# Second layer as sixteen lagged rounds, with sums of probabilities on TensorE and their reciprocal on VectorE

## The chip, the cores and the metric

One core of a Trainium2 chip. The metric is the time of one execution of the whole program on the device, in microseconds (us); lower is better. Three runs of the kernel before took 2073.58, 2075.54 and 2075.81 us (median 2075.54).

## The reference

Three things are computed one after the other on x of 8 batches x 256 x 512, in float32: a first cross-attention layer with its own network; a second layer (the one that changes), which is a self-attention block and then a cross-attention block over `ctx_2048`; and a network. The second layer's attention, cut to what matters:

```python
def attention(q, k, v, mask):
    scores = einsum('bhqd,bhkd->bhqk', q, k) / sqrt(32)      # 16 heads of 32
    scores = scores * mask - 10000.0 * (1.0 - mask)
    probs = softmax(scores, axis=-1)
    return einsum('bhqk,bhkd->bhqd', probs, v)

h = layernorm(x) @ w_qkv            # 512 x 1536, self-attention, mask shared by the batches
x1 = x + attention(q, k, v, m_self) @ w_ao + b_ao
q = layernorm(x1) @ w_q; k, v = split(ctx @ w_kv)             # cross-attention, a mask per batch
x2 = x1 + attention(q, k, v, m_cross[b]) @ w_co + b_co
```

256 tokens per batch, so each (batch, block, head) has a 256 x 256 matrix of probabilities.

## The kernel before

The program builds three parts in turn: `first_layer` (tiles named a_), `attention_layer` (b_) and `network_layer` (c_). A block of instructions per engine is written out by hand, with semaphores between them; each engine works its own queue strictly in order. Only `attention_layer` is changed.

**Units.** A unit is four heads by 128 queries: 8 units for a batch in one block, 128 in all. A unit goes through: `scores` (TensorE, L1281, four matmuls of 96 stacked rows: q and k are split into a high and a low float32r part, written to DRAM by `put` and read back stacked by `stack`), `soften` (VectorE: L1499 times the mask out of PSUM, L1503 adds and takes the row maximum), `exponentials` (ScalarE, L1393, whose accumulator also gives the row's sum `esum`), `turn_probs` (TensorE, L1293, eight transposes), `keep` (ScalarE, L1405, copies them out of PSUM), `weigh` (TensorE, L1307, values times probabilities in four column strips of the array; then L1312 spreads the reciprocals of the sums over 128 x 128 by a matmul with the identity), `invert` (VectorE, L1511, reciprocal of 4 sums) and `divide` (VectorE, L1521 copies the spread reciprocals out, L1523 multiplies).

**Order.** A loop body stands for one batch, with sixteen positions p. At each position every engine does one step of three or four different units (scores of unit p+2, transposes of p, `weigh` of p-1) and one item of `FILL`: a bank's worth of projections, layer-norm transposes or output projection for another batch. The self units of batch i+1 and i+2 alternate with the cross units of batch i: a body holds 8 of either kind. Projections are plain float32: `project` (L1219, eight matmuls of 256 columns a bank) and `by_token` (L1227, four of 512 columns a bank). A float32 matmul stands in the records as two instructions, so the counts of rows on such lines are twice those of the code; a float32r one is one instruction.

**Buffers.** Four PSUM banks in turn for transposes, weighed values and fills, and four banks for the scores of two units (`score[:, u % 2]`). A bank is claimed anew when the reader of its use four places before is done (`claim`).

**The network after it** (c_) already works with float32r parts: each product of a high and low part is three matmuls (L1745 with 256 columns, L1759 with 512), the first times the low, the low times the first, and the two high ones.

Rows name an instruction by its line, its engine, what it writes `<-` what it reads, and partitions x elements.

Of the kernel before, what the change touches and what calls it, by code (L numbers as in the profile page):

```python
# [12 lines left out]
P = 128  # L13
BANK = 512
# [843 lines left out]
def attention_layer(nc, sems, hid, enc_in, masks, ident_in, W, mid_out, scratch):  # L858

    B, S, D = hid.shape
# [5 lines left out]
    HUGE = 3.0e38  # L868

# [8 lines left out]
    FIRST, LAST = -3, B  # L878
    POSITIONS = range(2 * NU)
# [6 lines left out]
    def there(b):  # L886
        return not isinstance(b, int) or 0 <= b < B

    def unit_at(i, p):

        if p < 0:
            return CROSS, i - 1, p + NU
        if p < NU:
            return SELF, i + 1, p
        if p < 2 * NU:
            return CROSS, i, p - NU
        return SELF, i + 2, p - 2 * NU

    def phase_before(a, b):
        if a == CROSS:  # L900
            return (CROSS, b - 1) if isinstance(b, int) and b == B - 1 else (SELF, b + 1)
        if isinstance(b, int) and b < 2:
            return (SELF, 0) if b == 1 else None
        return CROSS, b - 2

    def two_before(a, b, u):
        if u >= 2:
            return a, b, u - 2
        phase = phase_before(a, b)
        return phase and (*phase, u + NU - 2)  # L910

    def earlier(uses, at, step, i):

        while True:
            at -= step
            if at < 0:
                at, i = at + len(uses), i - 1
                if isinstance(i, int) and i < FIRST:
                    return None
            use, shift = uses[at]  # L920
            if use and there(i + shift):
                return use, i + shift

    with ExitStack() as ctx:
# [3 lines left out]
        def sig(name, per, unit=1):  # L928
            return Signal(sems, nc, "b_" + name, per, unit)

        wqkv = sb("wqkv", [P, KT, 3 * D])
        wkv = sb("wkv", [P, KT, 2 * D])
        wq2 = sb("wq2", [P, KT, D])
        wout = [sb(f"wout{a}", [P, KT, D]) for a in range(2)]
# [5 lines left out]
        bqs = sb("bqs", [P, 2, KT])  # L940
# [3 lines left out]
        mask = [sb(f"mask{a}", [P, TT, S]) for a in range(2)]  # L944
        minus = [sb(f"minus{a}", [P, TT, S]) for a in range(2)]
        xt = sb("xt", [P, TT, D])
        xb = sb("xb", [P, TT, D])
        x1 = sb("x1", [P, TT, D])
        x1b = sb("x1b", [P, TT, D])
        xn = sb("xn", [P, TT, D])  # L950
        enc = sb("enc", [P, TT, D])
        lnT = [sb(f"lnT{a}", [P, KT, S]) for a in range(2)]
        encT = sb("encT", [P, KT, S])
        stats = sb("stats", [P, 2, TT, 6])
        mv = sb("mv", [P, 2, TT, 2])
        vare = sb("vare", [P, 2, TT])
        rstd = sb("rstd", [P, 2, TT])
        full = [sb(f"full{s}", [P, KT, S]) for s in range(2)]
        parts = sb("parts", [P, 2, KT, S], F32R)
        qst = sb("qst", [ROWS, 2, HH, S], F32R)  # L960
        kst = sb("kst", [ROWS, 2, HH, S], F32R)
        val = [sb(f"val{a}", [P, TT, D]) for a in range(2)]
# [3 lines left out]
        esum = sb("esum", [P, NU, G])  # L966
        inverse = sb("inverse", [P, NU, G])
        spread = sb("spread", [P, 2, P])
        pt = sb("pt", [P, 2, TT, G * P])
        cxT = [sb(f"cxT{a}", [P, KT, S]) for a in range(2)]  # L970

        consts_in = sig("consts_in", 1, 16)
        qk_in = sig("qk_in", 1, 16)
        v_in = sig("v_in", 1, 16)
        mask0_in = sig("mask0_in", 1, 16)
        late_in = sig("late_in", 1, 16)
        x_in = sig("x_in", 1, 16)
        enc_load = sig("enc_load", 1, 16)
        mask_in = sig("mask_in", 1, 16)
        set_up = sig("set_up", 1)  # L980
        x_biased = [sig(f"x_biased{a}", 1) for a in range(2)]
        var_done = [sig(f"var_done{a}", 1) for a in range(2)]
        rstd_done = [sig(f"rstd_done{a}", 1) for a in range(2)]
        xn_done = [sig(f"xn_done{a}", 1) for a in range(2)]
        turn_filled = [sig(f"turn_filled{a}", 2) for a in range(2)]
        ln_done = [sig(f"ln_done{a}", KT) for a in range(2)]
        enc_filled = sig("enc_filled", 2)
        enc_done = sig("enc_done", 2)
        qk_filled = [sig(f"qk_filled{a}", 4) for a in range(2)]
        v_filled = [sig(f"v_filled{a}", TT) for a in range(2)]  # L990
        q_full = [sig(f"q_full{a}", KT) for a in range(2)]
        k_full = [sig(f"k_full{a}", KT) for a in range(2)]
        v_done = [sig(f"v_done{a}", TT) for a in range(2)]
        q_parts = [sig(f"q_parts{a}", 1) for a in range(2)]
        k_parts = [sig(f"k_parts{a}", 1) for a in range(2)]
        qk_out = [[sig(f"qk_out{a}{h}", 4, 16) for h in range(2)] for a in range(2)]
        stacked = [[sig(f"stacked{a}{h}", 2 * len(Q_PARTS), 16) for h in range(2)] for a in range(2)]
        score_filled = [sig(f"score_filled{a}", NU) for a in range(2)]
        masked = [sig(f"masked{a}", NU) for a in range(2)]
        max_done = [sig(f"max_done{a}", NU) for a in range(2)]  # L1000
        exp_done = [sig(f"exp_done{a}", NU) for a in range(2)]
        pt_filled = [sig(f"pt_filled{a}", NU * TT) for a in range(2)]
        pt_done = [sig(f"pt_done{a}", NU * TT) for a in range(2)]
        pv_done = [sig(f"pv_done{a}", NU) for a in range(2)]
        inverse_done = [sig(f"inverse_done{a}", NU) for a in range(2)]
        cx_done = [sig(f"cx_done{a}", NU) for a in range(2)]
        cxT_done = [sig(f"cxT_done{a}", KT) for a in range(2)]
        o_filled = [sig(f"o_filled{a}", TT) for a in range(2)]
        x_done = [sig(f"x_done{a}", TT) for a in range(2)]
# [4 lines left out]
            0: [(("turn", 0, u), 2) for u in range(2)],  # L1014
            1: [(("q", 0, 0), 2)],
            2: [(("o", 1, t_), -1) for t_ in range(TT)],
            3: [(("q", 0, 1), 2)],
            4: [(("k", 0, 0), 2)],
            5: [(("k", 0, 1), 2)],
            6: [(("v", 1, 0), 0)],  # L1020
            7: [(("v", 1, 1), 0)],
            8: [(("enc", u), 1) for u in range(2)],
            9: [(("k", 1, 0), 1)],
            10: [(("o", 0, t_), 1) for t_ in range(TT)],
            11: [(("k", 1, 1), 1)],
            12: [(("v", 0, 0), 2)],
            13: [(("turn", 1, u), 1) for u in range(2)] + [(("v", 0, 1), 2)],
            14: [(("q", 1, 0), 1)],
            15: [(("q", 1, 1), 1)],
        }  # L1030
        BANKS = 4
        uses = []
        for p in POSITIONS:
            a, shift, u = unit_at(0, p)
            uses += [(("pt", a, u, k), shift) for k in range(TT)]
            a, shift, u = unit_at(0, p - 1)
            uses += [(("w", a, u), shift)]
            uses += FILL[p]
        uses += [(None, 0)] * (-len(uses) % BANKS)
        place = {use: n for n, (use, _) in enumerate(uses) if use}  # L1040
        read = {("enc", u): (enc_done, u + 1) for u in range(2)}
        for a in range(2):
            read |= {("turn", a, u): (ln_done[a], 2 * u + 2) for u in range(2)}
            read |= {("q", a, u): (q_full[a], 2 * u + 2) for u in range(2)}
            read |= {("k", a, u): (k_full[a], 2 * u + 2) for u in range(2)}
            read |= {("v", a, t_): (v_done[a], t_ + 1) for t_ in range(TT)}
            read |= {("pt", a, u, k): (pt_done[a], u * TT + k + 1) for u in range(NU) for k in range(TT)}
            read |= {("w", a, u): (cx_done[a], u + 1) for u in range(NU)}
            read |= {("o", a, t_): (x_done[a], t_ + 1) for t_ in range(TT)}
# [3 lines left out]
        def bank(use):  # L1053
            return psum[:, place[use] % BANKS, :]

        def claim(eng, use, i):

            before = earlier(uses, place[use], BANKS, i)
            if before:
                signal, n = read[before[0]]  # L1060
                signal.need(eng, before[1], n)
            return bank(use)


        q_of = lambda a: (q_full[a], q_parts[a])
        k_of = lambda a: (k_full[a], k_parts[a])
        PUTS = [((1, "q"), 0), ((0, "q"), 2), ((0, "k"), 2), ((1, "k"), 1)]
        FULLS = [[((0, "q"), 2), ((1, "k"), 1)], [((0, "k"), 2), ((1, "q"), 1)]]
        XNS = [((1,), 1), ((0,), 3)]

        def of(use):
            return (q_of if use[1] == "q" else k_of)(use[0])

        def outs(use):
# [896 lines left out]
```

## Time and profile before

| | |
|---|---|
| median of three runs | 2075.54 us |
| the profiled execution | 2075.23 us, its span 2073.4 us (1.8 us lie outside the span) |
| TensorE busy | 1848.8 us, 89% of the span |
| VectorE busy | 1185.4 us, 57% |
| ScalarE busy | 1050.9 us, 51% |
| GpSimd busy | 138.0 us, 7% |
| granted TensorE clock, mean | 0.946 of full speed |
| the second layer (b_) | from 778.6 to 1674.4 us of the span, 895.8 us |

A busy share says how long the engine had an instruction in it. TensorE's matmuls overlap (the next starts before the last one's end), so what a group of matmuls costs the engine is the distance from its start to the start of the next group, and not its duration times its count. VectorE's instructions overlap a little too.

### The profile page before, as it was taken

The page shows a single profiled execution, that of the slowest core. Times are in us where ns is not written, and L with a number is a line of the kernel's source. Part 1 is how long each engine was busy: PE and PEld are TensorE (multiplying, and loading weights), DVE is VectorE, ACT ScalarE, POOL GpSimd, SP SyncE. Part 2 cuts the span into 40 slices and gives each one's busy share as a digit, 9 for nine tenths or more (in the row PEclk, how much of TensorE's full clock was granted, in tenths as well). Part 3 has the DMA queues.
Part 4 walks back from the last instruction along what each step waited for, and adds up shares of the span by engine and source line. Part 5 has one row for each costly group of instructions (what it writes and reads, how often), then busy time and mean ns, then how long its engine had stood idle before and what let it go on. Part 6 is the DMA issues. An engine that isn't in the chain of part 4 may idle for free. (4 is left out here: it accounts for less than half of the span.)

```text
span 2073.4 us, 32615 instructions
## 1 busy us (share of the span) xinstructions
PE 1848.8 (89%) x12032; PEld 1207.3 (58%) x12032; DVE 1185.4 (57%) x2735; ACT 1050.9 (51%) x2298; POOL 138.0 (7%) x95
## 2 busy tenths in 40 slices
PE   3779999999999864889999999999988749999999
PEld 2324344344443323657776776767656438999988
DVE  5667677676766311656767676766665536333332
ACT  1346666675665621546666666666665433111121
POOL 3010110110000000010001000000000000000000
PEclk7779999999999977799999999999999979999999
DMA  5222323222221008365545454455450333000000
GB/s 163 84 77 74 98 74 98 78 84 88 63 68 63 12 9 274 75 154 121 128 113 128 114 127 123 122 129 125 114 129 27 92 99 122 21 21 21 21 21 21
DMA packets 159374, 185.36 MB, mean 89 GB/s; under 512 B 25072, under 2 KB 115312, under 8 KB 159216
## 3 DMA queue, kind: packets, MB, share of 16 engines
q1 hardware_dynamic: 159216, 183.27, 32.5%
q8 instruction: 97, 1.59, 0.3%
q14 instruction: 61, 0.50, 0.1%
HBM read 119.78 MB, written 63.44 MB: 88 GB/s over the span
## 5 line engine op out<-in xcount | busy, mean ns | idle before, releaser
L733 DVE TENSOR_REDUCE a_mx<-a_mscore 128x2 f32<-128x1024 f32 x256 | 312.9, 1222 | 184.7 <-PE a_mscore L428 183.4
L1393 ACT ACTIVATE b_pr<-b_t,b_nmax 128x256 f32<-128x256 f32 x512 | 253.8, 499 | 182.5 <-DVE b_nmax L1503 182.5
L584 ACT ACTIVATE a_pt<-a_escore 128x1024 f32<-128x1024 f32 x256 | 262.5, 1025 | 163.4 <-PE a_escore L416 162.9
L1499 DVE TENSOR_TENSOR b_t<-b_score,b_mask 128x1024 f32<-128x1024 f32 x128 | 155.9, 1218 | 158.8 <-PE b_score L1281 158.8
L1503 DVE CUSTOM_DVE_ANT_0 b_t<-b_t,b_minus 128x256 f32<-128x256 f32 x512 | 196.7, 439 | 16.9
L1820 ACT ACTIVATE c_gT<-c_d,c_b 128x256 f32<-128x256 f32 x128 | 53.6, 470 | 264.2 <-PE c_d L1745 264.1
L1405 ACT ACTIVATE b_pt<-b_d 128x512 f32<-128x512 f32 x256 | 138.8, 591 | 75.9 <-PE b_d L1293 70.9
L1293 PE MATMUL b_d<-b_ident,b_pr 128*128 128x128 f32 x1024 | 142.4, 280 | 20.1 <-DVE b_cxT L1523 8.0
L416 PEld LDWEIGHTS a_escore<-a_qst,a_kst 50*128 50x128 f32 x512 | 49.6, 190 | 177.8 <-ACT a_pt L584 106.0
L416 PE MATMUL a_escore<-a_qst,a_kst 50*128 50x512 f32 x512 | 132.6, 514 | 22.7 <-ACT a_pt L584 22.5
L428 PE MATMUL a_mscore<-a_kst,a_qst 48*128 48x512 f32 x512 | 117.9, 454 | 36.1 <-DVE a_mx L733 26.5
L1745 PE MATMUL c_d<-c_ln_high,c_w_high 128*128 128x256 f32 x512 | 144.5, 282 | 4.1 <-DVE c_w_low L1870 4.1
L1745 PE MATMUL c_d<-c_ln_high,c_w_low 128*128 128x256 f32 x512 | 143.8, 281 | 0.0
L1745 PE MATMUL c_d<-c_ln_low,c_w_high 128*128 128x256 f32 x512 | 143.8, 281 | 0.0
L1855 DVE CAST c_g_high<-c_gT 128x512 fp32r<-128x512 f32 x64 | 38.8, 606 | 175.6 <-ACT c_gT L1820 175.6
L1293 PEld LDWEIGHTS b_d<-b_ident,b_pr 128*128 128x128 f32 x1024 | 118.0, 143 | 28.3 <-issue 9.5
L1281 PE MATMUL b_score<-b_kst,b_qst 96*128 96x256 f32 x512 | 114.2, 347 | 19.7 <-DMA b_kst<-b_k 19.2
L445 PE MATMUL a_d<-a_pt,a_vaug 128*32 128x512 f32 x1024 | 130.8, 632 | 0.0
L1219 PE MATMUL b_d<-b_lnT,b_wqkv 128*128 128x256 f32 x512 | 125.9, 402 | 3.5 <-ACT b_full L1355 1.9
L1227 PE MATMUL b_d<-b_wout,b_cxT 128*128 128x512 f32 x256 | 115.6, 605 | 6.3 <-ACT b_cxT L1383 5.2
L1219 PEld LDWEIGHTS b_d<-b_lnT,b_wqkv 128*128 128x128 f32 x512 | 99.8, 200 | 24.4 <-issue 4.5
L1307 PE MATMUL b_d<-b_pt,b_val 128*32 128x128 f32 x2048 | 84.2, 283 | 30.6 <-ACT b_lnT L1340 12.7
(137 smaller groups left out, 3252.2 us busy)
## 6 DMA issues: line engine op xcount, KB each, us to landing
b_qst<-b_q SPq DMA_DIRECT2D x96, 256.0 KB, 5.0
b_kst<-b_k SPq DMA_DIRECT2D x96, 256.0 KB, 7.1
b_q<-b_parts SPq DMA_DIRECT2D x64, 256.0 KB, 2.8
b_k<-b_parts SPq DMA_DIRECT2D x64, 256.0 KB, 2.8
a_qst<-a_q_parts SPq DMA_DIRECT2D x192, 64.0 KB, 2.2
a_kst<-a_k_parts SPq DMA_DIRECT2D x192, 64.0 KB, 2.2
a_k_parts<-a_kparts SPq DMA_DIRECT2D x32, 256.0 KB, 2.3
a_q_parts<-a_qparts SPq DMA_DIRECT2D x32, 256.0 KB, 2.4
```

The source lines that it names most:

```text
L416: mm = nc.tensor.matmul(escore[:, e, :], kst[rows, pair, k * P:(k + 1) * P], qst[rows, pair, :], start=True, stop=True)
L428: mm = nc.tensor.matmul(mscore[:, e, :], qst[rows, pair, q * P:(q + 1) * P], kst[rows, pair, :], start=True, stop=True)
L445: mm = nc.tensor.matmul(at[32 * j:32 * j + 32, :], vaug[:, k, GROUP * g + j, :], pt[:, (b * UNITS + pair * TT + k) % RING, e, :], start=(k ...
L584: nc.scalar.activation(pt[:, at % RING, :, :], escore[:], ACT.Exp, scale=SCALE).then_inc(exp_done.sem, 1)
L733: nc.vector.tensor_reduce(mx[:, q, 2 * pair:2 * pair + 2], mscore[:], AX_X, ALU.max).then_inc(max_done.sem, 1)
L1219: mm = nc.tensor.matmul(at[:, j * S:(j + 1) * S], w[:, k, m:m + P], src[:, k, :], start=(k == 0), stop=(k == KT - 1))
L1293: last = nc.tensor.transpose(at[:, j * P:(j + 1) * P], pr[:, u % 2, j, k * P:(k + 1) * P], ident[:])
L1393: last = nc.scalar.activation(pr[:, u % 2, j, :], t[:, u % 2, j, :], ACT.Exp, scale=-1.0, bias=nmax[:, u, j:j + 1], accum_out=esum[:, u, j ...
L1405: nc.scalar.activation(pt[:, u % 2, k, :], bank(("pt", a, u, k)), ACT.Copy).then_inc(pt_done[a].sem, 1)
L1499: nc.vector.tensor_tensor(t[:, u % 2], score[:, u % 2].rearrange("p x (y n) -> p (x y) n", y=2), mask[a][:, q, :].unsqueeze(1).broadcast_t ...
L1503: last = nc.vector.tensor_tensor_reduce(t[:, u % 2, j, :], t[:, u % 2, j, :], minus[a][:, q, :], -1.0, HUGE, ALU.add, ALU.min, accum_out=n ...
L1745: mm = nc.tensor.matmul(bank[:, j * S:(j + 1) * S], w1[w][:, k, m:m + P], lnp[v][:, k, :], start=(k == 0 and n == 0), stop=(k == KT - 1 an ...
```

## The change

`attention_layer` is written anew; the computation is the same.

- **Rounds.** There are sixteen rounds of eight units: first the self block of all 8 batches, then the cross block of all 8. The result of the self block goes to `mid_out` in DRAM and comes back. Everything for a round lags it by fixed distances: layer norm two rounds ahead, projections one to two rounds ahead, output projection one round behind. Each round loads its input twice (`xt` for the norm, `xr` for the residual, which GpSimd adds the bias to).
- **Projections** use float32r parts and three products in place of one float32 product. The weights are split once (four for self, four later for cross, in `WEIGHTS_AT`), the normed input in every round (`turned_high` on ScalarE, `turned_low` on VectorE), the encoder states in the cross rounds (`encoded`, `encoded_low`), the context before the output projection (`context_high`, `context_low`), and q and k right out of PSUM (`high`, `low`).
- **Sums.** `exponentials` drops the accumulator. `weigh` takes two units at a time; after the values it multiplies the same transposed probabilities by a block of ones, so that the row sums appear spread over the strips. `divide` takes the reciprocal of 256 such numbers per partition straight from PSUM and multiplies. `invert` and the matmuls with the identity (L1312) are gone.
- **Buffers.** Six PSUM banks in turn; two banks for scores, of one unit (`scores` of a unit waits until VectorE has read those of the unit before). Three slots for transposed probabilities.

The core of the diff:

```diff
         FILL = {
-            0: [(("turn", 0, u), 2) for u in range(2)],
-            1: [(("q", 0, 0), 2)],
...
+            0: [("q", 1, 1)],
+            1: [("k", 1, 1)],
+            2: [("v", 0, 1)],
+            3: [("v", 1, 1), ("turn", 0, 2), ("turn", 1, 2)],
+            4: [("o", 0, -1)],
+            5: [("enc", 0, 2), ("enc", 1, 2), ("o", 1, -1)],
+            6: [("q", 0, 2)],
+            7: [("k", 0, 2)],
...
-        BANKS = 4
+        BANKS = 6
...
-        score = ctx.enter_context(nc.psum_tensor("b_score", [P, 2, 2, BANK], F32))
+        score = ctx.enter_context(nc.psum_tensor("b_score", [P, 2, BANK], F32))
...
+        WEIGHTS_AT = {(FIRST, 3): 0, (FIRST, 5): 1, (FIRST + 1, 0): 2, (FIRST + 1, 2): 3,
+                      (B - 2, 1): 4, (B - 2, 4): 5, (B - 2, 7): 6, (B, 6): 7}
...
                     for k in range(KT):
-                        mm = nc.tensor.matmul(at[:, j * S:(j + 1) * S], w[:, k, m:m + P], src[:, k, :],
-                                              start=(k == 0), stop=(k == KT - 1))
+                        for c, (x, y) in enumerate(((0, 0), (0, 1), (1, 0))):
+                            mm = nc.tensor.matmul(at[:, j * S:(j + 1) * S], w[:, x, k, m:m + P], src[:, y, k, :],
+                                                  start=(k == 0 and c == 0), stop=(k == KT - 1 and c == 2))
...
+                for x in range(2):
+                    u = 2 * pair + x
+                    for k in range(TT):
+                        for j in range(G):
+                            mm = nc.tensor.matmul(at[j * DH:(j + 1) * DH, (2 + x) * P:(3 + x) * P], ones[:],
+                                                  pt[:, slot(v, u), k, j * P:(j + 1) * P],
+                                                  start=(k == 0), stop=(k == TT - 1), tile_position=(0, j * DH))
...
-                nc.vector.tensor_copy(spread[:, u % 2, :], at[:, P:2 * P])
+                at = bank("w", v, pair).rearrange("p (x n) -> p x n", x=4)
+                nc.vector.reciprocal(spread[:, pair % 2], at[:, 2:4, :])
                 nc.vector.drain()
-                nc.vector.tensor_tensor(cxT[a][:, 2 * h + four, q * P:(q + 1) * P], at[:, 0:P], spread[:, u % 2, :],
-                                        ALU.mult).then_inc(cx_done[a].sem, 1)
+                nc.vector.tensor_tensor(cx[:, 2 * h:2 * h + 2, q * P:(q + 1) * P], at[:, 0:2, :], spread[:, pair % 2],
+                                        ALU.mult).then_inc(cx_done.sem, 1)
```

The order of a round on VectorE, which the prediction follows (`v` is the round, p its position):

```python
for p in range(NU):
    soften(*unit_at(v, p + 2))
    if p == 0: low(v + 1, 1, 0)
    if p == 1: low(v + 1, 0, 1); normalise(v + 2); context_low(v - 1, 1)
    if p == 2: low(v + 1, 1, 1); apply(v + 2)
    if p == 4: set_mask(v + 1)
    if p == 5: turned_low(v + 2); residual_sum(v - 1, 0)
    if p == 6: residual_sum(v - 1, 1); encoded_low(v + 2)
    if p == 7: low(v + 2, 0, 0); context_low(v, 0)
    if p % 2 == 0: divide of the pair of units p - 2, p - 1
    if (v, p) in WEIGHTS_AT: low_weight(...)
```

## Rows read from the trace of the kernel before

**Rows 1.** The page: busy us, share of the span and instructions of each engine
```profile
PE 1848.8 (89%) x12032; PEld 1207.3 (58%) x12032; DVE 1185.4 (57%) x2735; ACT 1050.9 (51%) x2298; POOL 138.0 (7%) x95
```

**Rows 2.** Stretches: us; busy PE, PEld, DVE, ACT, POOL; clock, DMA share, GB/s
```profile
778.60:1674.40 895.80, 796.20 (x6336) 580.10 (x6336) 558.50 (x1755) 530.97 (x1585) 48.95 (x33) 0.95 0.48 121
1029.60:1533.30 503.70, 480.47 (x3937) 352.42 (x3936) 345.39 (x1088) 328.83 (x984) 29.90 (x19) 0.99 0.50 123
```

**Rows 3.** Timeline of VectorE: the cross residual of batches 0 and 5
```profile
1029.63 0.69 DVE L1535 TENSOR_TENSOR b_x1b<-b_d,b_x1b 128x512 f32<-128x512 f32 x1 [1.89 <-PE b_d L1227]
...
1533.34 0.69 DVE L1535 TENSOR_TENSOR b_x1b<-b_d,b_x1b 128x512 f32<-128x512 f32 x1 [5.04 <-PE b_d L1227]
```

**Rows 4.** The longest wait of TensorE from 1000 to 1500 us
```profile
PE b_d L1307 <- ACT b_lnT L1340: 10.4, 10, 1.7
```

**Rows 5.** Timeline of TensorE, one position of a steady batch (start, length)
```profile
1106.43 0.83 PE L1281 MATMUL b_score<-b_kst,b_qst 96*128 96x256 f32 x4
1107.10 1.04 PE L1293 MATMUL b_d<-b_ident,b_pr 128*128 128x128 f32 x8
1108.07 0.64 PE L1307 MATMUL b_d<-b_pt,b_val 128*32 128x128 f32 x16
1108.53 0.40 PE L1312 MATMUL b_d<-b_ident,b_inverse 128*32 128x128 f32 x8
1108.86 3.72 PE L1219 MATMUL b_d<-b_lnT,b_wq 128*128 128x256 f32 x16
1112.23 0.83 PE L1281 MATMUL b_score<-b_kst,b_qst 96*128 96x256 f32 x4
```

**Rows 6.** Timeline of TensorE in the network: where 24 and then 12 matmuls begin and end
```profile
1851.94 0.28 PE L1745 MATMUL c_d<-c_ln_high,c_w_high 128*128 128x256 f32 x1
...
1854.77 0.39 PE L1759 MATMUL c_sums<-c_w_high,c_g_high 128*128 128x512 f32 x1
...
1857.57 0.28 PE L1745 MATMUL c_d<-c_ln_high,c_w_high 128*128 128x256 f32 x1
```

**Rows 7.** Timeline of VectorE, most of the same position
```profile
1107.30 1.22 DVE L1499 TENSOR_TENSOR b_t<-b_score,b_mask 128x1024 f32<-128x1024 f32 x1 [1.63 <-PE b_score L1281]
...
1110.04 0.29 DVE L1521 COPY b_spread<-b_d 128x128 f32<-128x128 f32 x1
1110.40 0.29 DVE L1523 TENSOR_TENSOR b_cxT<-b_d,b_spread 128x128 f32<-128x128 f32 x1
1110.61 0.17 DVE L1511 RECIPROCAL b_inverse<-b_esum 128x4 f32<-128x4 f32 x1
1110.70 0.97 DVE L1468 TENSOR_SCALAR b_xn<-b_xt,b_mv,b_rstd 128x512 f32<-128x512 f32 x2
```

**Rows 8.** Groups by line and shape (count; busy us, mean ns of one; idle before)
```profile
L1393 ACT ACTIVATE b_pr<-b_t,b_nmax 128x256 f32<-128x256 f32 x512 | 253.8, 499 | 182.5 <-DVE b_nmax L1503 182.5
L1486 DVE TENSOR_TENSOR b_parts<-b_full,b_parts 128x1024 fp32r<-128x1024 f32 x32 | 39.2, 1225 | 2.4
L1511 DVE RECIPROCAL b_inverse<-b_esum 128x4 f32<-128x4 f32 x128 | 21.5, 168 | 0.0
L781 DVE TENSOR_TENSOR a_ctxt<-a_d,a_rsum 128x256 f32<-128x256 f32 x32 | 13.6, 425 | 2.4
L778 DVE RECIPROCAL a_rsum<-a_d 128x16 f32<-128x16 f32 x32 | 7.8, 245 | 26.6 <-PE a_d L454 26.6
L1450 DVE BATCH_NORM_STATS2 b_stats<-b_xt 128x6 f32<-128x512 f32 x16 | 10.1, 674 | 0.0
L1745 PEld LDWEIGHTS c_d<-c_ln_high,c_w_low 128*128 128x128 f32 x512 | 97.2, 190 | 0.0
```

**Rows 9.** The tile b_minus: shortest, median and longest of a line, ns
```profile
L1503 DVE CUSTOM_DVE_ANT_0 b_t<-b_t,b_minus x512: 412/421/2099, 833.8 to 1658.1; 128x256 f32<-128x256 f32 x171
```

**Rows 10.** Timeline of TensorE: first scores of the layer, and its last output projection
```profile
831.19 2.08 PE L1281 MATMUL b_score<-b_kst,b_qst 96*128 96x256 f32 x8 [12.80 <-DMA b_kst<-b_k]
...
1666.49 7.13 PE L1227 MATMUL b_d<-b_wout,b_cxT 128*128 128x512 f32 x16 [1.33 <-ACT b_cxT L1383]
```

More of the change, by code:

```diff
@@ L877, in attention_layer, with kind, batch, there @@
     SELF, CROSS = 0, 1
-    FIRST, LAST = -3, B
-    POSITIONS = range(2 * NU)
+    ROUNDS = 2 * B
+    FIRST, LAST = -2, ROUNDS
+    def kind(v):
+        return v // B
+    def batch(v):
+        return v % B
+    def there(v):
+        return 0 <= v < ROUNDS
     def unit(u):
@@ L1272, in scores @@
+            def scores(v, u):
+                if not there(v):
                     return
@@ new lines, in _, with body @@
+            pe.wait_ge(consts_in.sem, 16 * CONSTS)
+            ones_set.need(pe, 0, 1)
+            def body(v):
+                for p in range(NU):
+                    scores(*unit_at(v, p + 2))
+                    turn_probs(*unit_at(v, p))
+                    if p % 2 == 0:
+                        w, u = unit_at(v, p - 2)
+                        weigh(w, u // 2)
+                    fill(v, p)
+            for v in range(FIRST, LAST + 1):
+                body(v)
+        @block.scalar
@@ new lines, in context_low, with residual_sum @@
+            def context_low(v, h):
+                if not there(v):
+                    return
+                cx_high.need(dve, v, h + 1)
+                for k in range(2 * h, 2 * h + 2):
+                    last = nc.vector.scalar_tensor_tensor(cxp[:, 1, k, :], cx[:, k, :], value_bias(kind(v), k),
+                                                          cxp[:, 0, k, :].bitcast(F32), ALU.add, ALU.subtract)
+                last.then_inc(cx_low.sem, 1)
+            def residual_sum(v, t_):
+                if not there(v):
@@ L1409, in _, with body @@
-            act.wait_ge(set_up.sem, 2)
-            def body(i):
-                for p in POSITIONS:
-                    keep(*unit_at(i, p))
-                    exponentials(*unit_at(i, p + 2))
+                    r_biased.need(dve, v, 1)
+                o_filled.need(dve, v, t_ + 1)
+                nc.vector.tensor_tensor(xr[:, t_, :], bank("o", v, t_), xr[:, t_, :], ALU.add).then_inc(x_done.sem, 1)
+            dve.wait_ge(consts_in.sem, 16 * CONSTS)
+            def body(v):
+                for p in range(NU):
+                    soften(*unit_at(v, p + 2))
@@ L1578, in network_layer @@
+                    if p % 2 == 0:
+                        w, u = unit_at(v, p - 2)
+                        divide(w, u // 2)
+                    if (v, p) in WEIGHTS_AT:
+                        low_weight(WEIGHTS_AT[v, p])
+            for v in range(FIRST, LAST + 1):
+                body(v)
 def network_layer(nc, sems, mid_in, ident_in, W, out):
```

1012 lines of the change are left out of this document (502 added, 510 removed).

## The prediction

> **What bounds the kernel now.** I read the page first, then the busy time by stretch, the waits, and the timelines of TensorE and VectorE over one position. The page says TensorE: 89% of the span against 57% for VectorE [rows 1]. An average over three parts does not say what the changed part waits for, so the stretches come next. The second layer takes 895.8 us, and in five steady batches TensorE is busy 480.5 of 503.7 us, at a clock of 0.99, with VectorE at 345 and ScalarE at 329 [rows 2]. A batch takes (1533.34 - 1029.63)/5 = 100.7 us [rows 3]. The longest wait of TensorE in that stretch is 10.4 us in ten pieces, on ScalarE [rows 4]. The layer is bound by the instructions of TensorE; the other two engines wait for it.
>
> One position shows what they cost, by start to start [rows 5]: scores 0.67, eight transposes 0.97, weighted values 0.46, the spreading of the reciprocals 0.33, one bank of projections 3.37. That is 2.43 for a unit and 3.37 for a fill; a bank of 512 columns costs about the same (two take 7.13 with the last one's tail, [rows 10]). A batch has 16 units, 16 fills and three pairs of banks of norm or encoder transposes at about 0.9: 38.9 + 54 + 2.7 = 95.7 us. Measured are 100.7, so some 5 us a batch, 2.5 for a block of eight units, are waits and gaps, in agreement with the 23.2 us of idle time in five batches.
>
> **TensorE after the change.** The network shows the new form of projection: 24 float32r matmuls of 256 columns, which is one bank of `project` with its three products, take 1854.77 - 1851.94 = 2.83 us, and twelve of 512 columns, one bank of `by_token`, 2.80 us [rows 6]. So a fill falls from 3.37 to 2.82 although it has three products. The block of ones costs as much as the values do, 0.46 a unit (same probabilities, same strips, same count), in place of 0.33. A round then is 8 x 1.64 for scores and transposes, 4 x 1.84 for pairs in `weigh`, 8 x 2.82 for fills and 0.9 for norm transposes: 13.1 + 7.4 + 22.5 + 0.9 = 43.9 us, and 44.8 where encoder transposes are due. Two rounds are 88.7 against 95.7: 7.0 us a batch, 56 us over eight.
>
> **VectorE after the change.** By start to start `soften` takes 1110.04 - 1107.30 = 2.74 [rows 7], eight of them 21.9. New is `low` out of PSUM, eight instructions of 256 columns; the nearest row is a tensor_tensor of that size at 425 ns [rows 8], and as instructions overlap by some 0.08 (the copy and the multiply in rows 7 follow such ends), 0.34 each: 2.7. `context_low` is four of them, 1.4. `turned_low` is one of 128x1024 at 1.23, less the overlap 1.14 [rows 8]. The two residual sums are 1.2, a norm 1.9 (two of 674 ns and small ones), `apply` 0.97 [rows 7, 8]. The cross rounds add 1.2 for the encoder's low part and 1.0 for two passes over a mask. GpSimd's bias addition, once a round, can hold VectorE: its longest L1503 is 2099 against a median of 421 ns [rows 9], so 0 to 1.7 us a round, and I take 1.3. Since a copy, a reciprocal of 4 and a split in two passes go away, only `divide` is left.
>
> **The reciprocal** is the price that no row has: 256 numbers per partition out of PSUM, four times a round. The rows have 168 ns for 4 and 245 ns for 16 [rows 8]. From below it can't be under the tensor_tensor of the same width, 0.43 us. The slope, 77/12 = 6.4 ns an element, gives 245 + 240 x 6.4 = 1.78 us. From above, all of the 245 put on its 16 elements is 15.3 ns each, 3.9 us. I take 1.78, since both rows lie on it, and the multiply after it with its gap is 0.41: a `divide` is 2.19, a round 8.8. VectorE's round is then 21.9 + 8.8 + 2.7 + 1.4 + 1.1 + 1.2 + 1.9 + 1.0 + 1.3 = 41.3, and 43.5 in cross rounds: 1.3 to 2.6 under TensorE's. The Trainium skill (VectorE: DVE Perf Modes, "Walkthrough: the 8-slice pipeline in each mode") says that a reciprocal iterates its divide step with a repeat count of 8. At the clock that page gives, 0.96 GHz, I estimate 8.3 ns an element, a reciprocal of 2.25 us and VectorE's rounds 1.9 us longer, as long as TensorE's. The slope of the rows is 6.4, a little under it.
>
> **Why TensorE still leads.** With one pair of score banks, TensorE may fill unit p+2 only when L1499 of p+1 has read them. L1499 stands first in VectorE's position, so VectorE may lag by a position less some 2 us before TensorE stops. Positions 1 and 2 are VectorE's long ones (2.74 + 0.7 + 1.9 + 0.7 = 6.0 against 4.5; then 6.6 against 6.3), position 3 its short one (2.7 against 5.3): the lag grows to about 2 and is gone again. Six banks give the readers 1.7 positions where four gave one. ScalarE loses the accumulator reads and gains the high parts; its exponentials of 32 x 0.5 and the copies leave it under 40 us a round. SP's queue has more loads, but a stack is ordered five positions (some 27 us) before it is read. So I keep the 2.5 us of waits per round and add 0.5, because two engines are now close: 46.9 and 47.8 us.
>
> **The sum.** The start waits for the first stack: scores at 831.2 [rows 10]. After it, splitting weights and parts costs a little and writing half of q and k at a time saves it; I leave 831 and add two positions at low clock, 9: 61.5 us to round 0. Round 0 has no output projection, 41. Rounds 1 to 5: 5 x 46.9 = 234.5. Round 6 splits three weights, 6 x 1.14 = 6.8 more on VectorE, 41.3 + 1.2 + 6.8 = 49.3 and waits: 52. Round 7 is 47.8, round 8, with one weight, 49.5, rounds 9 to 13 239. Round 14 has six fills, 40.5; round 15 two, VectorE's, 30. The last division, context parts, two banks and the residual: 14. Together 810 us against 895.8: 86 us less, more than the 56 of the matmuls, because the ends are shorter: before, the first batch is done 251 us after the layer's start (1029.6 - 778.6) and the last two take 141 us (1674.4 - 1533.3, [rows 2, 3]), 392 us for three batches of 95.7. The other parts are untouched. The profiled execution took 2075.2, 0.3 under the median, so 2075.2 - 86 = 1989.
>
> **The rivals.**
> *The reciprocal is steeper, and VectorE sets the rounds.* At 8.3 ns an element, as the estimate above has it, 1.9 us more a round; its rounds (43.2, 45.4) meet TensorE's, and I count 1.5 us of new waits in 14 rounds: 21, so 2010. For it speaks that the 4-element reciprocal is 168 ns and short instructions may share a floor, which would hide part of the slope; against it that 16 cost only 245.
> *Only the matmuls count.* If the start and end are no shorter, 56 us: 2019.
> *The waits halve.* Six banks and paired weighing may remove 1.8 of the 3.0 us of waits a round: 14 x 1.8 = 25, so 1964.
> *Lock step (the other side).* `divide` waits for `weigh`, which waits for ScalarE's copies; the next `soften` stands behind `divide`, and the next scores, having one buffer, behind `soften`. Positions would then last VectorE's work plus TensorE's scores and L1499's first part: about 0.7 more in even positions, 1.5 in odd ones, some 8 us a round, 128 in all: 2117. It turns the sign from 5.4 us a round (86/16). Against it is the lag worked out above, and that L1499 waited for scores on TensorE, not the reverse [rows 7].
> *Weight loads become visible.* 24 loads of 0.19 [rows 8] in sequence would be 4.56 a bank, 128 x 1.74 = 223 us more, 2212; the network has the same loads in 2.83 [rows 6].
>
> **How the numbers follow.** The forecast 0.42, the steeper reciprocal 0.2, halved waits 0.14, matmuls alone 0.11, lock step 0.08, loads 0.03, nothing gained 0.02. Under 0.2% (4 us) a measurement of this kernel can't be told from no change. Faster: 0.42 + 0.2 + 0.14 + 0.11 = 0.87, same 0.02, slower 0.11. The range reaches from below the halved waits, 1955, over the two slower gains to 2035, which takes in a reciprocal up to 2.7 us (0.45 more, four times a round, in 14 rounds, beyond 2010). A reciprocal at its upper end, 3.9 us, lies beyond: VectorE's rounds would be 50 to 52 us, with waits 6 more than forecast in 14 rounds, about 2075.
>
> **What would show it.** L1219 and L1227's successors as 2.8 us between bank starts; ones as long as values; the reciprocal at 1.8 us; rounds of 47 to 48 us between residual sums; VectorE busy near 88% in the layer and TensorE's waits not on L1499. Wrong would be a reciprocal over 3 us, TensorE idle before scores in every round, or a start or end longer than 61 and 85 us.

## The result

The changed kernel takes 1958.88 us (median of four runs, 1954.23 to 1961.46) against 2075.68 (2073.58 to 2078.21): a ratio of 0.9434, 95% interval 0.9414 to 0.9455, 117 us faster. The forecast was 1989 in a range of 1955 to 2035. The profiled execution took 1954.23, its span 1952.5 us: 121.0 us less than the profiled one before. Of these 118.8 lie in the second layer. Of all executions below one, at 3591.21 us where the three others of its kernel took 1991.89 to 1998.66, is in no median and no ratio.

The page after, to be laid beside [rows 1]:

```profile
PE 1760.3 (90%) x13824; PEld 1268.8 (65%) x13824; DVE 1312.3 (67%) x2662; ACT 1024.2 (52%) x1818; POOL 140.7 (7%) x96
```

Stretches of the layer after (columns as in [rows 2]): the whole, the time to the start of round 0, round 0, rounds 1 to 5, rounds 6, 7 and 8, rounds 9 to 13, round 15 with the tail. I take a round as beginning at the scores of its position 0.

```profile
777.30:1554.30 777.00, 709.18 (x8128) 641.03 (x8128) 683.54 (x1682) 504.26 (x1105) 51.92 (x34) 0.97 0.59 161
...
777.30:830.40 53.10, 30.36 (x193) 28.44 (x194) 26.15 (x51) 21.82 (x35) 1.51 (x4) 0.73 0.77 215
830.40:869.20 38.80, 36.75 (x419) 34.06 (x418) 35.17 (x99) 29.86 (x67) 0.69 (x1) 0.96 0.57 150
869.20:1085.20 216.00, 214.09 (x2522) 194.63 (x2521) 199.75 (x511) 149.25 (x336) 16.30 (x10) 1.00 0.61 165
1085.20:1138.30 53.10, 47.38 (x515) 42.18 (x514) 47.16 (x109) 34.60 (x74) 3.26 (x2) 0.94 0.64 179
1138.30:1187.40 49.10, 44.61 (x515) 39.80 (x514) 44.86 (x110) 32.81 (x72) 3.27 (x2) 1.00 0.64 178
1187.40:1233.30 45.90, 43.82 (x514) 39.74 (x513) 43.42 (x104) 32.11 (x70) 3.24 (x2) 1.00 0.62 167
1233.30:1465.20 231.90, 219.18 (x2563) 199.01 (x2562) 214.69 (x537) 155.41 (x347) 16.50 (x10) 1.00 0.61 166
...
1503.80:1554.30 50.50, 36.87 (x456) 30.85 (x456) 36.82 (x84) 22.62 (x50) 4.70 (x2) 0.86 0.09 33
```

A round of rounds 1 to 5 lasts 43.2 us, with TensorE busy for 42.8 and VectorE for 40.0. One of rounds 9 to 13 lasts 46.4 (43.8 and 42.9 busy). VectorE, at 62% of the layer before, is now at 88%. Ten steady rounds take 447.9 us where five steady batches took 503.7 [rows 2], 55.8 less. The rest of the layer, 392.1 before, takes 329.1: 63.0 less.

TensorE after, two positions of a self round, the first with a `weigh`; as in [rows 5], start to start is the price:

```profile
988.18 0.64 PE L1284 MATMUL b_score<-b_kst,b_qst 96*128 96x256 f32 x4
988.66 1.04 PE L1296 MATMUL b_d<-b_ident,b_pr 128*128 128x128 f32 x8
989.63 1.08 PE L1313 MATMUL b_d<-b_pt,b_val 128*32 128x128 f32 x32
990.53 1.06 PE L1320 MATMUL b_d<-b_pt,b_ones 128*32 128x128 f32 x32
991.52 3.10 PE L1223 MATMUL b_d<-b_lnp,b_wq 128*128 128x256 f32 x24
994.46 0.64 PE L1284 MATMUL b_score<-b_kst,b_qst 96*128 96x256 f32 x4
994.93 1.04 PE L1296 MATMUL b_d<-b_ident,b_pr 128*128 128x128 f32 x8
995.73 3.09 PE L1223 MATMUL b_d<-b_lnp,b_wk 128*128 128x256 f32 x24
998.65 0.52 PE L1284 MATMUL b_score<-b_kst,b_qst 96*128 96x256 f32 x3
```

The reader is to see no idle note in brackets, a bank at 2.94 and 2.92, ones (0.99) about as long as values (0.90), and the scores at 0.48 where they took 0.67 before. The transposes take 0.97 ahead of values and 0.80 ahead of a bank.

The reciprocal, by the tile b_spread (shortest, median, longest in ns):

```profile
L1580 DVE RECIPROCAL b_spread<-b_d x64: 1737/1747/1758, 845.0 to 1540.6; 128x256 f32<-128x256 f32 x64
```

TensorE's longest waits from 900 to 1450 us (total, times, longest), and one of them in the timeline of a cross round:

```profile
PE b_d L1223 <- DVE b_encp L1522: 8.7, 6, 1.5
PE b_d L1296 <- DVE b_kparts L1539: 7.0, 7, 1.5
PE b_d L1231 <- ACT b_val L1404: 3.8, 9, 0.6
```

```profile
1362.00 1.06 PE L1320 MATMUL b_d<-b_pt,b_ones 128*32 128x128 f32 x32
1364.51 3.08 PE L1223 MATMUL b_d<-b_lnp,b_wq 128*128 128x256 f32 x24 [1.45 <-DVE b_encp L1522]
```

These are claims of banks. q's bank at position 6 is the one that enc 0 filled six uses earlier, at position 5. VectorE reads that last, in `encoded_low`, behind `soften` and a residual sum of position 6.

The first scores of the layer and the last output projection, as in [rows 10]:

```profile
819.44 0.73 PE L1284 MATMUL b_score<-b_kst,b_qst 96*128 96x256 f32 x4 [0.92 <-DMA b_kst<-b_k]
...
1545.71 7.88 PE L1231 MATMUL b_d<-b_wo,b_cxp 128*128 128x512 f32 x24 [5.21 <-DVE b_cxp L1590]
```

### The profile page after: what moved, and what is told of

It reads as the page before. It is cut to its first block and busy times, and to the rows that moved or that the text cites. A ratio compares the mean times of both kernels' runs of the same rounds, so it can differ in the third digit from the quotient of the medians.

```text
span 1952.5 us, 35589 instructions
## 1 busy us (share of the span) xinstructions
PE 1760.3 (90%) x13824; PEld 1268.8 (65%) x13824; DVE 1312.3 (67%) x2662; ACT 1024.2 (52%) x1818; POOL 140.7 (7%) x96
## 5 line engine op out<-in xcount | busy, mean ns | idle before, releaser
L1425 ACT ACTIVATE b_pr<-b_t,b_nmax 128x256 f32<-128x256 f32 x512 | 218.9, 501 | 182.9 <-DVE b_nmax L1568 182.6
L1564 DVE TENSOR_TENSOR b_t<-b_score,b_mask 128x1024 f32<-128x1024 f32 x128 | 156.0, 1219 | 28.5 <-PE b_score L1284 28.5
L1296 PE MATMUL b_d<-b_ident,b_pr 128*128 128x128 f32 x1024 | 137.9, 277 | 9.8 <-DVE b_kparts L1539 7.0
L1223 PE MATMUL b_d<-b_lnp,b_wq 128*128 128x256 f32 x768 | 102.4, 291 | 16.2 <-DVE b_encp L1522 10.2
L1580 DVE RECIPROCAL b_spread<-b_d 128x256 f32<-128x256 f32 x64 | 111.9, 1749 | 4.1 <-PE b_d L1320 3.6
L1223 PEld LDWEIGHTS b_d<-b_lnp,b_wq 128*128 128x128 f32 x768 | 96.2, 195 | 22.6 <-issue 20.0
L1231 PE MATMUL b_d<-b_wo,b_cxp 128*128 128x512 f32 x384 | 98.9, 408 | 9.5 <-DVE b_cxp L1590 5.2
L1818 PE MATMUL c_sums<-c_w_high,c_g_high 128*128 128x512 f32 x256 | 101.7, 397 | 3.0 <-DVE c_w_low L1929 3.0
```

The source lines that it names most:

```text
L1223: mm = nc.tensor.matmul(at[:, j * S:(j + 1) * S], w[:, x, k, m:m + P], src[:, y, k, :], start=(k == 0 and c == 0), stop=(k == KT - 1 and c ...
L1296: last = nc.tensor.transpose(at[:, j * P:(j + 1) * P], pr[:, u % 2, j, k * P:(k + 1) * P], ident[:])
L1425: last = nc.scalar.activation(pr[:, u % 2, j, :], t[:, u % 2, j, :], ACT.Exp, scale=-1.0, bias=nmax[:, u, j:j + 1])
L1564: nc.vector.tensor_tensor(t[:, u % 2], score[:].rearrange("p x (y n) -> p (x y) n", y=2), mask[s][:, q, :].unsqueeze(1).broadcast_to([P, G ...
L1818: mm = nc.tensor.matmul(sums[:, t_, :], gp[v][:, u % RING, at:at + P], w2[w][:, k, :], start=(k == 0 and n == 0), stop=(k == FT - 1 and n ...
```

## The experiments

After this profile I held that a self round lasts what TensorE's instructions last and a cross round what VectorE's do: theory 1 of the expectations. The theories numbered beside it place the length, or the source of the gain, elsewhere: theory 2 has VectorE set all rounds, theory 3 has TensorE set all of them, its idle time included. Ratios are to the kernel before on the same chip, with their 95% intervals; "us" without a name are medians. Each edit is made to the changed kernel unless it says otherwise.

**One float32 product per projection** (the splitting of inputs and weights still runs; the low parts go unused, and the high ones stand for the inputs):

```diff
-for c, (x, y) in enumerate(((0, 0), (0, 1), (1, 0))):
-    mm = nc.tensor.matmul(..., w[:, x, k, m:m + P], src[:, y, k, :], ...)
+mm = nc.tensor.matmul(..., w[:, 0, k, m:m + P].bitcast(F32), src[:, 0, k, :].bitcast(F32), ...)
```

> The changed kernel with each projection as one plain float32 product of the high parts; the splitting and all else stay (the low parts are left out of the products). Theory 1 (TensorE sets the self rounds, VectorE the cross rounds and rounds 6 and 7): a bank goes from 2.94 to 3.37 us, eight a round, so self rounds go from 43.2 to 46.7 us and cross rounds, where TensorE now has 2 to 3 us idle, up by 1 to 2: about 40 us more, 1999. Theory 2 (VectorE sets all rounds): under 10 us more. Theory 3 (TensorE sets all rounds, its idle time is latency): 16 x 3.5 = 56 more, 2015.

Measured 2019.07 us, 0.9724 (0.9704 to 0.9745): 60 us are lost. Self rounds last 47.6 to 47.9 with TensorE idle at most 0.2. Its timeline:

```profile
1014.64 3.72 PE L1222 MATMUL b_d<-b_lnp,b_wq 128*128 128x256 f32 x16
1018.01 0.83 PE L1282 MATMUL b_score<-b_kst,b_qst 96*128 96x256 f32 x4
1018.68 1.04 PE L1294 MATMUL b_d<-b_ident,b_pr 128*128 128x128 f32 x8
```

The banks are back at 3.37 and 3.27 (2.94 and 2.92 before the edit), and the scores behind them at 0.67. A position costs (3.37 - 2.94) + (0.67 - 0.48) = 0.62 more, a round of eight 5.0. Nearly a third of what the float32r form saves stands on another line, in the scores. The time is that of theory 3 (2015) and not of theory 1 (1999), which had the cross rounds only 1 to 2 us longer: rounds 9 to 13 went from 46.4 to 50.0.

**Accumulator and identity back** (`exponentials` with `accum_out`, `invert`, the spread by the identity; `divide` copies):

```diff
-mm = nc.tensor.matmul(at[...], ones[:], pt[:, slot(v, u), k, j * P:(j + 1) * P], ...)
+mm = nc.tensor.matmul(at[...], inverse[:, u, j:j + 1].broadcast_to([P, DH]), ident[:], ...)
...
-nc.vector.reciprocal(spread[:, pair % 2], at[:, 2:4, :])
+nc.vector.tensor_copy(spread[:, pair % 2], at[:, 2:4, :])
```

> The sums as before the change in the new order: ScalarE accumulates them, VectorE takes the reciprocals of eight, TensorE spreads them with the identity, VectorE copies 256 out. TensorE 1.3 us a round less, VectorE 4 x 1.33 less and 0.5 more for the small reciprocal, ScalarE 6 us more with 13 idle. Theory 1: self rounds 1.3 less, cross rounds 3.5 less, rounds 6 and 7 5 less: about 40 us less than the changed kernel, 1918. Theory 2: 4.8 a round, 77 less, 1882. Theory 3: 21 less, 1938.

Measured 1932.60, 0.9309 (0.9288 to 0.9329): 26 us faster than the changed kernel. The block of ones with its wide reciprocal is a loss. The tile b_spread there:

```profile
L1586 DVE COPY b_spread<-b_d x64: 406/414/425, 847.5 to 1517.3; 128x256 f32<-128x256 f32 x64
```

1.75 us become 0.41, and the spread by the identity takes TensorE 0.55 us for two units:

```profile
996.28 0.62 PE L1320 MATMUL b_d<-b_ident,b_inverse 128*32 128x128 f32 x16
996.83 3.10 PE L1223 MATMUL b_d<-b_lnp,b_wq 128*128 128x256 f32 x24
```

The ones took 0.99, so a round has 4 x 0.44 = 1.8 us less on TensorE, where the expectation had 1.3. Self rounds fall to 41.2 to 42.2, and cross rounds 9 to 13 to 45.7 on average. Of the expectations theory 3's 1938 is nearest, theory 1's 1918 too low: it had the cross rounds 3.5 us shorter, and they are 0.7 shorter.

**A copy in place of the reciprocal** (the division is left out; the ones stay):

```diff
-nc.vector.reciprocal(spread[:, pair % 2], at[:, 2:4, :])
+nc.vector.tensor_copy(spread[:, pair % 2], at[:, 2:4, :])
```

> VectorE copies the sums out of PSUM in place of taking their reciprocal, so the division is left out; all else as changed. VectorE has 5.3 us a round less. Theory 1: self rounds as they are, cross rounds 2 to 2.5 less, rounds 6 and 7 up to 5 less: about 25 less, 1934. Theory 2: 85 less, 1875. Theory 3: no change over 4 us.

Measured 1941.71, 0.9349 (0.9329 to 0.9368): 17 us. VectorE has 5.3 us less to do in a round (4 x 1.33), yet the five self rounds together shorten by only 1.9, and four of them last 42.58 with TensorE never idle: TensorE's length, as theories 1 and 3 said and theory 2 did not. Cross rounds 9 to 13 shorten by only 0.8 on average although VectorE then idles 8.2 us in each (187.1 of 228.0 busy). They are not VectorE's length, and theory 1's 2 to 2.5 us for each of them, and with that its 25 us in all, were too much.

**No ones matmuls** (the reciprocal reads the weighed values instead, so sums are left out):

```diff
-mm = nc.tensor.matmul(at[...], ones[:], pt[:, slot(v, u), k, j * P:(j + 1) * P], ...)
...
-nc.vector.reciprocal(spread[:, pair % 2], at[:, 2:4, :])
+nc.vector.reciprocal(spread[:, pair % 2], at[:, 0:2, :])
```

> The matmuls with the block of ones are left out, and the reciprocal is taken of the weighted values, so the sums are left out of the result; VectorE's work is the same. TensorE has 4 x 0.99 us a round less. Theory 1: self rounds fall only to VectorE's own length, some 1.7 less, cross rounds under 0.5: 10 to 15 less, 1946. Theory 2: under 10 less. Theory 3: 64 less, 1895.

Measured 1952.75, 0.9408 (0.9391 to 0.9425): 6 us by the medians, 5 by the ratios, where theory 1 had 10 to 15 and theory 3 64. Only theory 2's "under 10" fits this number, and the copy, which took 5.3 us of VectorE's work out of a round and shortened the self rounds by 0.4, speaks against it. Rounds 1 to 5:

```profile
868.10:1080.90 212.80, 198.53 (x1883) 176.91 (x1882) 200.41 (x511) 148.99 (x335) 16.31 (x10) 1.00 0.63 167
```

They last 42.6 in place of 43.2. TensorE is busy for (214.09 - 198.53)/5 = 3.1 us less in each, and idle for (212.80 - 198.53)/5 = 2.9, VectorE for 2.5. By the waits of this stretch TensorE waits 6.6 us for the low part of k on VectorE and 6.4 for ScalarE to read v's banks. What is taken from TensorE alone turns into waits for banks, as what was taken from VectorE alone did into idle time there. The cross rounds even grow. Rounds 9 to 13 last 47.1 us in place of 46.4, with TensorE idle for 4.8 in each (2.5 with the ones in place) and a granted clock of 0.96 in place of 1.00:

```profile
1231.76:1467.27 235.51, 211.67 (x1923) 189.66 (x1921) 213.34 (x531) 155.05 (x346) 16.58 (x10) 0.96 0.59 163
```

The accumulator's version takes from both engines, and its rounds are the shorter ones.

**Four banks and two pairs of score banks**, as in the kernel before:

```diff
-BANKS = 6
+BANKS = 4
...
-score = ctx.enter_context(nc.psum_tensor("b_score", [P, 2, BANK], F32))
+score = ctx.enter_context(nc.psum_tensor("b_score", [P, 2, 2, BANK], F32))
...
-before = units_before(1, v, u)
+before = units_before(2, v, u)
```

> The changed kernel with the PSUM banks as before it: four in turn, and scores of two units. Theory A (six banks took away the waits that the kernel before had, 2.5 us a round): self rounds from 43.2 to about 45.7 and cross rounds from 46.1 to 48, 35 us more, 1994. Theory B (the new order of the steps did it; four banks do as well, since the second pair of score banks gives slack elsewhere): within 8 us of 1959.

Measured 2123.57, 1.0229 (1.0211 to 1.0247): 165 us lost, slower than the kernel before. Its layer, five microseconds of a cross round, what TensorE does there, and its longest waits in three cross rounds (1322 to 1506):

```profile
778.00:1720.00 942.00, 762.50 (x8128) 679.59 (x8128) 689.09 (x1682) 511.19 (x1105) 52.51 (x34) 0.91 0.48 133
```

```profile
1403.80:1408.80 5.00, 5.00 (x23) 4.13 (x22) 2.82 (x4) 0.87 (x3) 0.00 (x0) 0.66 0.30 105
```

```profile
1403.06 4.62 PE L1231 MATMUL b_d<-b_wv,b_encp 128*128 128x512 f32 x12 [4.24 <-DVE b_kparts L1539]
```

```profile
PE b_d L1231 <- DVE b_kparts L1539: 11.9, 3, 4.2
PE b_d L1296 <- DVE b_encp L1522: 11.0, 3, 3.7
PE b_d L1212 <- DVE b_xr L1600: 10.0, 3, 3.3
PE b_d L1223 <- DVE b_kparts L1539: 3.4, 3, 1.3
```

Theory A had 35 us and theory B at most 8; the loss is far beyond both. With the same 8128 matmuls, TensorE is idle 179.5 us instead of 67.8 and busy 53.3 longer. Idle time makes 111.7 of the 165, and the lower clock is what the trace shows for the rest: behind 4.24 idle us the granted clock of the next stretch is 0.66, a mean over its two levels (1.2 and 2.4 GHz), and twelve matmuls last 4.62 us that take 3.05 five us later at 1.00. From the mean clocks of the layer, 0.97 and 0.91, I estimate 709 x (0.97/0.91 - 1) = 47 us. The run has both buffer edits in it; the waits listed are all claims of banks, none is for the scores. The changed kernel needs the six banks. With four, a bank is claimed about a position after it was filled, while its reader stands two or three instructions deep in VectorE's queue.

**Both arithmetic parts undone** (the first two edits together; order and buffers of the changed kernel):

> Both changes of arithmetic undone, rounds and buffers kept: one plain float32 product a projection (the low parts left out of it) and the sums by accumulator and identity. If the parts add up: 60 more for the products and 26 less for the sums, 1993, so that the order and the buffers alone are worth 82 us of the 117. If TensorE's length alone counts (the sums save it 1.3 us a round and the products cost 4.7): 16 x 3.4 = 54 more, 2013.

Measured 1994.61, 0.9612 (0.9596 to 0.9629), the median of three runs. The parts add up: 1958.88 + 60.2 - 26.3 = 1992.8. So order and buffers bring 81 us, the products 62 (1932.60 against 1994.61), ones and reciprocal cost 24 to 26. Most of the 81 lies at the ends and the turn from self to cross: rounds 1 to 5 and 9 to 13 of this run take 476.7 us against the 503.7 of five batches before, 27 less. What in the order makes the rest, no run separates.

**The accumulator's version with the output projection ahead of the encoder transposes:**

```diff
-5: [("enc", 0, 2), ("enc", 1, 2), ("o", 1, -1)],
+5: [("o", 1, -1), ("enc", 0, 2), ("enc", 1, 2)],
```

> The sums as in the run with the accumulator, and at position 5 the output projection goes ahead of the two banks of encoder transposes, so that the projection of q at position 6 claims the bank of the output projection and not that of a transpose whose low part VectorE has not read. Theory: this claim is the 1.5 to 1.9 us that TensorE waits once in a cross round; eight rounds, 12 less, 1920. Rival (cross rounds are as long as VectorE's or ScalarE's queue, and the wait only moves): within 4 us of 1932.

Measured 1920.66, 0.9254 (0.9241 to 0.9266), the fastest version of the same computation, 38 us under the changed kernel. q's bank now claims that of o 1, whose reader, the residual sum, comes earlier. TensorE's waits in the steady cross rounds, first of the version without the edit, then with it:

```profile
PE b_d L1223 <- DVE b_encp L1521: 9.4, 5, 1.9
PE b_d L1296 <- DVE b_kparts L1538: 6.1, 5, 1.6
```

```profile
PE b_d L1223 <- DVE b_xr L1606: 6.3, 5, 1.3
PE b_d L1296 <- DVE b_kparts L1538: 4.4, 5, 1.6
```

No instruction was added or taken away, and cross rounds 9 to 13 fell from 45.7 to 44.1 us, 7.8 in all. Of these 4.8 are idle time of TensorE (15.6 to 10.8) and 3.1 busy time (212.81 to 209.75) at a mean clock of 0.99 without the edit and 1.00 with it. Their length is that of TensorE's instructions plus the waits for single banks: 209.75 busy us and these two waits, 10.7, make up the five rounds' 220.57. The cross half of theory 1 fell here.

**The same edit alone in the changed kernel:**

> The changed kernel (block of ones, reciprocal of 256) with the output projection ahead of the encoder transposes at position 5. The claim that TensorE waits for, 1.45 us a cross round, goes away. Theory (TensorE's wait is local, VectorE has room): 8 to 12 less, 1949. Rival (with the long reciprocal VectorE's queue is as long as the cross round, so the wait moves): within 4 us of 1959.

Measured 1950.02, 0.9404 (0.9386 to 0.9422): 9 us by the medians, 6 by the ratios, whose intervals overlap (0.9414 to 0.9455 without the edit). In the traces rounds 9 to 13 go from 46.4 to 46.1 only, and part of the wait moves: q's bank costs 5.1 us there in place of 8.7, the low part of k 4.4 in place of 3.4. The clock is 1.00 in both, so no busy time comes back. Between theory and rival this run does not decide; that VectorE's fuller queue is why the swap is worth less here is argued.

**The fastest version with `normalise(v + 2)` at position 0** instead of 1:

> As the run with the swapped transposes, and the norm's statistics (1.9 us of VectorE) move from position 1 to position 0. Theory: position 1 and 2 are where VectorE falls behind TensorE (6.0 us of work in a position of 4.2), and the transposes of position 3 then wait for the low part of k to free a bank, 1.2 to 1.6 us in about half the rounds: 10 less than the swap alone, 1910. Rival: the lag is absorbed anyway, within 4 us.

Measured 1928.50, 0.9293 (0.9280 to 0.9305): 8 us slower, a miss. Self rounds shorten by about 0.4 (to 41.6), but cross rounds 9 to 13 lengthen from 44.1 to 44.9. New is a wait of VectorE for the input that comes back from `middle`:

```profile
DVE b_stats L1494 <- DMA b_xt<-middle: 8.1, 5, 2.6
```

That is 4 us in five rounds. In the profiled execution round 0 also starts 4.7 us later (835.4 against 830.7), without a cause that I can name: among kernels whose start is alike it lies between 830.1 and 835.0. So the wait is not shown to be the whole loss.

**The kernel before with six banks** and one pair of score banks:

```diff
-BANKS = 4
+BANKS = 6
...
-before = two_before(a, b, u)
+before = one_before(a, b, u)
```

> The kernel before with the buffers of the changed one alone: six PSUM banks in turn, two banks for the scores of one unit. Theory A (the buffers took the waits away, in either order): TensorE's waits of 2.5 us a block of eight units go down to 0.5, eight batches: 30 less, 2045. Theory B (the old order had been laid out for four banks, and the buffers matter only with the new one, where four cost 165 us): within 8 us of 2075. Theory C (one pair of score banks is a loss there): slower by over 10.

Measured 2056.22, 0.9899 (0.9875 to 0.9923): 21 us by the ratio, 18 by the medians, between theories A and B. Its TensorE still waits for ScalarE's `b_lnT` as long as [rows 4] show, now ahead of the projections (from 1000 to 1500 us):

```profile
PE b_d L1225 <- ACT b_lnT L1346: 10.0, 5, 2.0
PE b_d L1225 <- ACT b_encT L1378: 5.8, 5, 1.2
```

In these 500 us TensorE is idle for 16.4, and for 20.2 in the kernel before. Of the 81 us of order and buffers the buffers alone give about a quarter in the old order. The changed kernel is a loss without them, so neither can be credited with the sum.

**The fastest version without the cross block's weights** (neither loaded nor split; the self block's are used again):

> On the run with the swapped transposes: the four weights of the cross rounds are neither loaded nor split, the cross rounds use those of the self rounds (so their weights are left out). Theory: that work, done in rounds 6 to 8 on ScalarE and VectorE, is what makes round 6 8 us and round 7 3 us longer than their neighbours: 12 less, 1909. Rival (it is the turn from self to cross, mask and encoder): within 4 us of 1921.

Measured 1912.64, 0.9218 (0.9202 to 0.9233), 8 us less. Rounds 6 and 7, with the weights and without:

```profile
1076.60:1175.80 99.20, 87.88 (x899) 78.46 (x898) 82.93 (x225) 72.75 (x209) 8.19 (x4) 0.97 0.67 184
```

```profile
1076.30:1163.80 87.50, 83.91 (x899) 75.98 (x898) 73.92 (x219) 67.35 (x203) 6.58 (x4) 1.00 0.65 173
```

The change of weights costs 11.7 us there, 7.7 as idle time of TensorE and 4.0 as busy time for the same 899 matmuls, at a clock of 0.97 in place of 1.00. Without it rounds 6 and 7 last 44.0 and 43.5, no longer than the cross rounds behind them, so the turn from self to cross itself costs nothing more. The profiled executions differ by 10.8 us, the medians by 8.

**The fastest version with each weight split by halves** at two positions:

> On the run with the swapped transposes: the same weights are split one half at a time, at positions 2, 3, 5, 6, 7 and 0 in place of whole at 1, 4 and 7. If the cost of the splitting is the lag that 2.3 us in one piece makes: half of it comes back, 5 less, 1916. If it is the work itself or the loads' arrival: within 3 us of 1921.

Measured 1924.73, 0.9276 (0.9260 to 0.9292): 4 us slower, a miss, with intervals that overlap. Round 6 lasts 52.9 instead of 51.8: spreading VectorE's split doesn't shorten it. The projection of q now waits 3.6 us there for the residual sum, 1.2 without the edit; that the half split at position 5, ahead of that sum in VectorE's queue, does it is argued.

## Why the prediction was nearly right, point by point

| stage | forecast | measured |
|---|---|---|
| start, to round 0 | 61.5 | 53.1 |
| round 0 | 41 | 38.8 |
| rounds 1 to 5 | 234.5 | 216.0 |
| rounds 6 to 8 | 149.3 | 148.1 |
| rounds 9 to 13 | 239 | 231.9 |
| round 14 | 40.5 | 38.6 |
| round 15 and tail | 44 | 50.5 |
| the layer | 810 | 777.0 |

- **TensorE bounds the layer before, and a fill falls to 2.82: right, a little low.** It is 2.93. But the shares were not those of the sum. Its 56 us are some 70 for the products (128 banks x 0.55) less some 17 for the ones. Measured, the products are worth 60 to 62, by about 0.4 a bank and 0.19 in each group of scores, and ones and reciprocal cost 24 to 26: 36 us together. Order and buffers, which the sum had at 86 - 56 = 30 for the shorter ends, bring 81. That 86 came as near to 117 as it did is in part luck: one share was 20 too high, the other 51 too low.
- **The scores at 0.67: too high.** TensorE's self round was to have 43.9 us of work and has 42.8: scores 8 x 0.19 and four transposes x 0.17 less, fills 8 x 0.11 and pairs 4 x 0.05 more, together -1.1.
- **The waits, "I keep the 2.5 us of waits per round and add 0.5": this step failed, and it is most of the miss in the self rounds.** Measured are (216.00 - 214.09)/5 = 0.4 us in a self round and (231.90 - 219.18)/5 = 2.5 in a cross round. The 2.5 of before was no fixed price of a round: six banks take away a fifth of the idle time even in the old order (20.2 to 16.4 us in 500), and in the self rounds of the new order nearly all of it is gone. They were carried over though the text ahead of that step named the six banks as a help. (These give the readers 1.5 to 1.6 positions, not 1.7: a round claims 30 or 32 banks in eight positions.) In rounds 1 to 5 this is 5 x 2.6 = 13 us, in rounds 9 to 13 2.5.
- **VectorE 1.3 to 2.6 us under TensorE: right in size.** Its self round was put at 41.3. With 2.5 to 3.3 us between its instructions, 40.0 busy us fill a round of 42.6 to 43.2 nearly to the end. It is busy for 88% of the layer, as forecast.
- **The reciprocal at 1.78 us: right**, at 1.747. From the 16 elements at 245 ns it is (1747 - 245)/240 = 6.26 ns an element. The Trainium skill (VectorE: DVE Perf Modes, "Walkthrough: the 8-slice pipeline in each mode") would, its repeat count of 8 read as eight cycles an element, have made it 2.25, an estimate; this case's trace, at 1.747, doesn't bear that reading out.
- **Ones as long as values: right.** That the pair of ones and wide reciprocal is a loss as a whole, 26 us, the sum contained (more TensorE, more VectorE) but did not say. The change's gain hid it.
- **Round 6 at 52, with three weights: right**, 53.1. TensorE waits 3.1 us for VectorE there and 2.6 for ScalarE's exponentials, and the weights cost what the last runs show.
- **The start, 8.4 us too long:** the first scores come at 819.4, not 831 (819.2 to 824.1 in the profiles of the runs that share this start). That half of q and k is written at a time is the argued cause; no run separates it. **Round 15 and the tail, 6.5 us too short:** round 15, up to its last `weigh` at 1538.12, lasts 34.3 in place of 30, with TensorE waiting 5.45 and 1.97 us for VectorE to read the scores (L1564). The end is 16.2 in place of 14: the last banks wait 5.21 us for the context's low part, a chain with no other work beside it.
- **Of the 33 us** between 810 and 777.0: waits in ten steady rounds 15.5, TensorE's work there 10, start 8.4, rounds 0, 6 to 8 and 14 5.3, round 15 and tail -6.5.

Of the rivals, *the waits halve* (1964) came nearest, and as a mechanism in the self rounds: its 1.8 us a round are 2.6 there and 0.5 in cross rounds. *The steeper reciprocal* is refuted by its row. *Visible weight loads* are refuted by 24 matmuls in 2.93. *Lock step* did not occur in the full rounds: TensorE waited on L1564 for its scores once in 900 to 1450, for 1.9 us. It did at the end, where a round has few or no fills between the scores: 9.9 us in three waits from 1465 on, of 13.9 in the whole layer.

```profile
1514.43 1.19 PE L1284 MATMUL b_score<-b_kst,b_qst 96*128 96x256 f32 x4 [5.45 <-DVE b_t L1564]
```

That the fills keep this rival away in the full rounds is argued from there. And the order can go over to the other side, at another place than I put it: not at the single pair of score banks but at the depth of the bank rotation, 165 us with four.

Open stay: why the scores behind a float32 bank are later by 0.19, whether the waits for the low part of k can be removed, what shortened the start, and what in the order brings the part of the 81 us that lies outside the steady rounds.

## What to carry to other kernels

Take each wait of the old profile by name and ask whether the change removes its cause, before it is carried over as a number a round; in a rotation of banks, list for each claim which use it claims and how deep that use's last reader stands in its engine's queue, for a swap of two fills was worth 12 us in the version with the accumulator and two banks fewer cost 165. When a change has several parts, undo each in its new surroundings: this one gained 117 us with a part in it that lost 26. Sums spread over a block cost a reciprocal for every copy of them; four reciprocals of sums a unit and a spread of the result did the same for less.

## What the hardware showed that I had not expected

- A float32 bank also delays what follows: four float32r matmuls of the scores take 0.67 us start to start behind one, and 0.48 behind a float32r bank.
- A reciprocal from PSUM costs 6.26 ns an element between 16 (245 ns) and 256 (1747 ns), and at 256 four times a copy of the same size (414).
- Waits cost twice: in the version with four banks, 111.7 us more of idle time came with 53.3 us more of busy time for the same matmuls, at a mean granted clock of 0.91 against 0.97.
- Less work can lengthen a stretch: without the ones TensorE's cross rounds had 4.8 us of idle time in place of 2.5, a clock of 0.96 in place of 1.00, and lasted 47.1 us in place of 46.4.
